# Edge numbers laid out on the host instead of turned on the chip, and the zeroing of the count matrix dealt out anew

## The reference

```
x = layernorm(x + sage(x, src, dst))        # two mean aggregations: h @ W_self + mean(h[src]) @ W_neigh + b
x = layernorm(x + mlp(x, edge_attr_64))     # message per edge: relu(relu([x[src], x[dst], attr] @ W1 + b1) @ W2 + b2), summed at dst
x = layernorm(x + gcn(x))                   # symmetric degree norm, self loops
x = layernorm(x + gin(x))                   # batch norm over the nodes
```

## Time and profile before

| what | value |
|---|---|
| median of 3 runs | 1707.18 us |
| the three runs | 1707.18, 1711.44, 1705.15 us |
| span of the profiled execution | 1708.6 us |
| end of phase 1 (first one-hot of the counting) | 27.80 us |
| end of the counting | 332.5 us |
| barrier before phase 5 | 498.5 us |
| busy in the span: PE, DVE, ACT, POOL | 1474.5, 753.7, 678.8, 773.8 us |
| mean granted TensorE clock | 0.949 of full |

### The profile page before, as it was taken

How to read it: one execution, slowest core, us unless ns; L and a number is a source line. 1 busy time by engine, 2 the same in 40 slices (tenths; PEclk the granted TensorE clock), 3 DMA queues, 4 the chain that set the end, 5 groups by cost and what they waited for, 6 DMA issues and landing times.

```text
span 1708.6 us, 31512 instructions
## 1 busy us (share of the span) xinstructions
PE 1474.5 (86%) x9804; PEld 1046.6 (61%) x9805; DVE 753.7 (44%) x2791; ACT 678.8 (40%) x1245; POOL 773.8 (45%) x821
## 2 busy tenths in 40 slices
PE   3789999999967877889898888889898888977997
PEld 2346666755555666667676667667666666654554
DVE  8987778622233322233234324333433343345445
ACT  7665555520012433344345334433444353331113
POOL 1300000000005777777777777777777777721000
PEclk9999999999987999989999999999999999988998
DMA  2000000000024333333333333333333333310001
GB/s 80 1 0 1 2 1 1 21 27 18 0 65 128 87 80 83 80 85 83 83 81 88 82 80 77 92 79 84 86 83 82 80 87 82 83 29 1 1 1 38
DMA packets 158749, 95.81 MB, mean 56 GB/s; under 512 B 120636, under 2 KB 143931, under 8 KB 158659
## 3 DMA queue, kind: packets, MB, share of 16 engines
q0 software_dynamic: 25088, 51.43, 11.9%
q1 hardware_dynamic: 133571, 43.21, 10.3%
HBM read 87.24 MB, written 7.32 MB: 55 GB/s over the span
## 4 chain that ended last, share of the span: by engine, by line
PE 33%; DMA 11%; POOL 9%; issue 7%; DVE 5%; DVEq 2%; ACT 2%; SPq 1%; POOLq 0%; ACTq 0%
DMA arena<-x_w1a,idx 10%; POOL arena L768 9%; PE ps L1093 6%; PE ps L1208 6%; PE ps L1102 5%; PE ps L1086 5%; PE ps L1074 3%; PE ps L1082 3%; PE ps L1143 2%; PE ps L1192 1%; DVEq L334 1%; DVE arena L2085 1%; DVE idx L2054 1%; DMA arena<-in_edge_attr 1%; ACT arena L1544 1%
## 5 line engine op out<-in xcount | busy, mean ns | idle before, releaser
L768 POOL DMA_INDIRECT arena<-x_w1a,idx x784 | 742.8, 947 | 684.1 <-issue 640.7
L1534 ACT ACTIVATE arena<-ps 88x512 f32<-88x512 f32 x196 | 116.2, 593 | 481.4 <-PE ps L1074 477.6
L1102 PEld LDWEIGHTS ps<-arena 128*128 128x128 f32 x1568 | 210.6, 198 | 111.8 <-issue 74.6
L2085 DVE TENSOR_TENSOR arena<-ps,bias_b 128x512 f32<-128x512 f32 x196 | 135.6, 692 | 208.1 <-PE ps L1093 208.1
L2080 DVE TENSOR_TENSOR arena<-win_i,late 128x96 f32<-128x96 f32 x196 | 51.1, 261 | 393.0 <-PE ps L1102 380.1
L1082 PE MATMUL ps<-ident_f,arena 128*128 128x128 f32 x784 | 131.2, 292 | 107.3 <-DMA arena<-x_w1a,idx 106.2
L1093 PE MATMUL ps<-w_c,arena 128*128 128x128 f32 x1568 | 222.2, 288 | 0.0
L1352 ACT ACTIVATE adj<-ps 128x300 f32 x392 | 172.1, 449 | 121.2 <-PE ps L831 114.4
L1086 PE MATMUL ps<-arena 88*128 88x512 f32 x392 | 210.1, 618 | 2.4 <-ACT arena L1534 2.4
L1093 PEld LDWEIGHTS ps<-w_c,arena 128*128 128x128 f32 x1568 | 205.4, 205 | 0.3
L1102 PE MATMUL ps<-arena 128*128 128x24 f32 x1568 | 199.3, 266 | 4.6 <-ACT arena L1544 1.4
(11 more groups left out here) (207 smaller groups left out, 1438.3 us busy)
## 6 DMA issues: line engine op xcount, KB each, us to landing
arena<-in_edge_attr SPq DMA_DIRECT2D x196, 128.0 KB
arena<-x_w1a,idx POOLq DMA_INDIRECT x784
arena<-x_w1b SPq DMA_DIRECT2D x196, 12.0 KB
x_spill<-arena SPq DMA_DIRECT2D x1, 1600.0 KB, 7.2
x_w1a<-arena SPq DMA_DIRECT2D x6, 256.0 KB, 2.3
x_w1b<-arena SPq DMA_DIRECT2D x6, 256.0 KB, 2.6
arena<-x_spill SPq DMA_DIRECT2D x6, 256.0 KB, 3.0
out_x<-arena SPq DMA_DIRECT2D x3, 512.0 KB
```

The costliest lines, as they stand in the source:

```text
L768: pool.indirect_dma_start(out=z_e[v][:, j * D:(j + 1) * D], out_offset=None, in_=xa_d[:, :], in_offset=bass.IndirectOffsetOnAxis(ap=idx[:, ...
L1102: last = pe.matmul(ps[:, WIN_BANK[v % 2], 0:WIN], msg[:, j * P:(j + 1) * P], oh_e[v][:, j, :], start=(j == 0), stop=(j == J - 1))
L2085: dve.tensor_tensor(msg.rearrange("p (j d) -> p j d", d=D), bank(5, J), over(bias_b, J), ALU.add).then_inc(m_sum[v], 1)
```

## The change

On the host, `src` and `dst` are padded to whole blocks and laid out with the edge position on the partitions, once for the counting and once for the later loop; first targets of half blocks, units and blocks are taken there too, and the node and edge features are padded with zero rows. On the chip, each of these is one transfer. The transposes, their copies, the store of the edge words and the patches of the last block go, and with them three semaphores. VectorE computes `high`, `low`, `rel`, `comb`, `lo_h` and the checks on 128 x 784 in place of 98 x 1024, and makes `drel` (the edge's target relative to its block) in phase 5 by one subtraction on 128 x 784. The raw numbers no longer stand in `adj`. Tiles are zeroed thus: VectorE 0 to 7 (was 0 to 6, 20, 21), ScalarE 8 to 16 (was 7 to 17, 22 to 24), GpSimd 17 to 24 in one instruction without a wait (was 18 and 19 behind `prep_ready`).

```diff
+def unit(q):
+    return 2 * (q // 4) + q % 2
+
+
+def unit_block(i, v, r):
+    return 2 * i + FB * r + FB * (v % 2) + v // 2
...
-        prep = adj[:, 20:25, :].rearrange("p k n -> p (k n)").bitcast(F32)
-        raw_src = prep[:, 0:1024].bitcast(I32)
-        raw_dst = prep[:, 1024:2048].bitcast(I32)
-        hi_i = prep[:, 2048:3072].bitcast(I32)
-        lo_i = prep[:, 3072:4096].bitcast(I32)
-        p_src = prep[:, 4096:5120]
-        p_lo = prep[:, 5120:6144]
-        p_drel = prep[:, 6144:7168]
-        p_comb = raw_dst.bitcast(F32)
-        p_rel = raw_src.bitcast(F32)
+        raw_src = arena[:, 10048:10048 + NB * J].bitcast(I32)
+        raw_dst = arena[:, 10832:10832 + NB * J].bitcast(I32)
+        high = arena[:, 11616:11616 + NB * J].bitcast(I32)
+        low = arena[:, 9024:9024 + NB * J].bitcast(I32)
+        rel = arena[:, 0:NB * J]
+        half_all = arena[:, 784:784 + HALVES].bitcast(I32)
...
-        edge_words = arena[:, 0:LATE]
-        src_words = edge_words[:, 0:J * (NB + 1)].bitcast(I32).rearrange("p (s j) -> p s j", j=J)
-        drel_words = edge_words[:, J * (NB + 1):LATE].rearrange("p (s j) -> p s j", j=J)
+        dst_words = late[:, J * (NB + 1):LATE].bitcast(I32)
+        base_all = arena[:, 10560:10560 + NB].bitcast(I32)
...
+        spans = [arena[0:1, 2800 + 200 * u:2800 + 200 * u + NB] for u in range(2)]
...
-            def block_rows(dst, src, s):
-                v = src[0:(NB - 1) * BLK].rearrange("(s e) -> s e", e=BLK)
-                sp.dma_start(dst[0:GRP, 0:512], v[0:GRP]).then_inc(s, 16)
-                sp.dma_start(dst[0:EVEN, 512:1024], v[GRP:GRP + EVEN]).then_inc(s, 16)
-                sp.dma_start(dst[EVEN:GRP - 1, 512:1024], v[GRP + EVEN:NB - 1]).then_inc(s, 16)
-                sp.dma_start(dst[GRP - 1:GRP, 512:1024],
-                             src[E - BLK:E].rearrange("(s e) -> s e", s=1)).then_inc(s, 16)
-
-            block_rows(raw_src, t["src"], loads[0])
-            block_rows(raw_dst, t["dst"], loads[1])
...
+            sp.dma_start(raw_src, t["src_counted"]).then_inc(loads[0], 16)
+            sp.dma_start(raw_dst, t["dst_counted"]).then_inc(loads[1], 16)
+            sp.dma_start(half_all, bcast(t["half_firsts"])).then_inc(loads[1], 16)
+            sp.dma_start(base_a, t["unit_firsts"]).then_inc(loads[2], 16)
+            sp.dma_start(base_row[:, :], t["block_firsts"].rearrange("(a s) -> a s", a=1)).then_inc(loads[2], 16)
 
             def load_nodes(dst, src, s):
-                sp.dma_start(dst[:, 0:NT - 1, :],
-                             src[0:(NT - 1) * P, :].rearrange("(k p) d -> p k d", p=P)).then_inc(s, 16)
-                sp.dma_start(dst[0:TAIL, NT - 1, :], src[(NT - 1) * P:N, :]).then_inc(s, 16)
-
-            sp.wait_ge(g_own, 1)
+                sp.dma_start(dst, src.rearrange("(k p) d -> p k d", p=P)).then_inc(s, 16)
+
             load_nodes(xn, t["x"], loads[3])
...
-            sp.wait_ge(loads[2], 112)
-            sp.wait_ge(prep_out, 8)
-            sp.wait_ge(prep_ready, 2)
-            sp.dma_start(late_d, edge_words).then_inc(words_moved, 16)
             phase_end(sp, 1)
             sp.wait_ge(adj_written, counted(ROUNDS))
-            sp.dma_start(late[:, :], late_d).then_inc(words_moved, 16)
+            sp.dma_start(base_all, bcast(t["block_firsts"])).then_inc(words_moved, 16)
+            sp.dma_start(dst_words, t["dst_edges"]).then_inc(words_moved, 16)
+            sp.dma_start(late[:, 0:J * (NB + 1)].bitcast(I32), t["src_edges"]).then_inc(words_moved, 16)
...
-            g.add(pool.memset(xn[:, NT - 1, :], 0.0))
...
-            pool.wait_ge(prep_ready, 1)
-            pool.memset(words(18, 20), 0)
+            pool.memset(words(17, 25), 0)
             phase_end(pool, 1)
...
-            pe.wait_ge(prep_ready, 1)
-            pe.wait_ge(g_own, 9)
-            n = 0
-            for half in range(2):
-                for a, v in enumerate((p_comb, p_lo, p_drel, p_src)):
-                    if n >= 2:
-                        pe.wait_ge(prep_out, n - 1)
-                    for j in range(J):
-                        c0 = 512 * half + j * P
-                        last = pe.transpose(ps[:, n % 2, GRP * j:GRP * (j + 1)], v[0:GRP, c0:c0 + P],
-                                            ident_f[0:GRP, 0:GRP])
-                    last.then_inc(prep_t, 1)
-                    n += 1
             phase_end(pe, 1)
...
-            zero(7, 12)
-            zero(12, 18)
-            for n in range(8):
-                half, a = n // 4, n % 4
-                dst = (comb, lo_h, drel_words, src_words)[a]
-                act.wait_ge(prep_t, n + 1)
-                act.activation(dst[:, GRP * half:GRP * (half + 1), :],
-                               ps[:, n % 2, 0:GRP * J].rearrange("p (j s) -> p s j", j=J), ACT.Copy
-                               ).then_inc(prep_out, 1)
-            zero(22, 25)
+            zero(8, 13)
+            zero(13, 17)
             phase_end(act, 1)
...
             dve.memset(cols[:, 6:7], 0.0).then_inc(cols_ready, 1)
             own.add(dve.memset(off[:, :], 0.0))
             dve.memset(words(0, 2), 0)
-            dve.wait_ge(loads[0], 64)
-            own.add(dve.tensor_scalar(hi_i[0:GRP, :], raw_src[0:GRP, :], 7, None, ALU.arith_shift_right))
-            own.add(dve.tensor_scalar(lo_i[0:GRP, :], raw_src[0:GRP, :], P - 1, None, ALU.bitwise_and))
-            own.add(dve.tensor_copy(p_src[0:GRP, :], raw_src[0:GRP, :]))
-            dve.wait_ge(loads[1], 64)
-            for half in range(2):
-                h = slice(512 * half, 512 * half + 512)
-                own.add(dve.tensor_scalar(p_drel[0:GRP, h], raw_dst[0:GRP, h],
-                                        raw_dst[0:GRP, 512 * half:512 * half + 1], None, ALU.subtract))
+            dve.wait_ge(loads[0], 16)
+            own.add(dve.tensor_scalar(high, raw_src, 7, None, ALU.arith_shift_right))
+            own.add(dve.tensor_scalar(low, raw_src, P - 1, None, ALU.bitwise_and))
+            dve.wait_ge(loads[1], 32)
+            firsts = half_all.rearrange("p (h a) -> p h a", a=1).broadcast_to([P, HALVES, J // 2])
+            own.add(dve.tensor_tensor(rel.rearrange("p (h j) -> p h j", j=J // 2),
+                                      raw_dst.rearrange("p (h j) -> p h j", j=J // 2), firsts, ALU.subtract))
             own.wait()
-            for h in range(4):
-                own.add(dve.tensor_scalar(p_rel[0:GRP, SUB * h:SUB * (h + 1)], raw_dst[0:GRP, SUB * h:SUB * (h + 1)],
-                                        raw_dst[0:GRP, SUB * h:SUB * h + 1], None, ALU.subtract))
-            firsts = raw_dst[0:GRP, :].rearrange("p (b h e) -> p b h e", h=2, e=SUB)[:, :, :, 0]
-
-            for c, x, y in ((4, 1, 0), (6, 0, 1)):
-                own.add(dve.tensor_tensor(off[0:GRP, c:c + 2], firsts[:, :, x], firsts[:, :, y], ALU.subtract))
-            own.add(dve.tensor_copy(p_lo[0:GRP, :], lo_i[0:GRP, :]))
-            own.wait()
-            dve.scalar_tensor_tensor(out=p_comb[0:GRP, :], in0=hi_i[0:GRP, :], scalar=float(WIN_A),
-                                     in1=p_rel[0:GRP, :], op0=ALU.mult, op1=ALU.add).then_inc(prep_ready, 1)
-            own.add(dve.tensor_reduce(off[0:GRP, 1:2], p_rel[0:GRP, :], mybir.AxisListType.X, ALU.max))
-            own.add(dve.tensor_reduce(off[0:GRP, 2:3], p_rel[0:GRP, :], mybir.AxisListType.X, ALU.min))
-            own.add(dve.tensor_scalar(off[0:GRP, 4:6], off[0:GRP, 4:6], float(WIN - WIN_A), None, ALU.subtract))
-            own.wait()
-            own.add(dve.tensor_scalar(off[0:GRP, 1:2], off[0:GRP, 1:2], WIN_A - 1.0, None, ALU.subtract))
-            own.add(dve.tensor_scalar(off[0:GRP, 2:3], off[0:GRP, 2:3], -1.0, None, ALU.mult))
-
-            dve.wait_ge(loads[2], 112)
+            own.add(dve.scalar_tensor_tensor(out=comb, in0=high.rearrange("p (s j) -> p s j", j=J), scalar=float(WIN_A),
+                                             in1=rel.rearrange("p (s j) -> p s j", j=J), op0=ALU.mult, op1=ALU.add))
+            own.add(dve.tensor_copy(lo_h, low.rearrange("p (s j) -> p s j", j=J)))
+            own.add(dve.tensor_reduce(off[:, 1:2], rel, mybir.AxisListType.X, ALU.max))
+            own.add(dve.tensor_reduce(off[:, 2:3], rel, mybir.AxisListType.X, ALU.min))
+            halves = half_all[0:1, :].rearrange("p (s h) -> p s h", h=2)
+            for u in range(2):
+                own.add(dve.tensor_tensor(spans[u], halves[:, :, 1 - u], halves[:, :, u], ALU.subtract))
+            dve.wait_ge(loads[2], 32)
             own.add(dve.tensor_tensor(falls, base_row[:, 0:NB - 1], base_row[:, 1:NB], ALU.subtract))
             own.add(dve.tensor_tensor(nears, base_row[:, 0:NB - APART], base_row[:, APART:NB], ALU.subtract))
             own.wait()
+            own.add(dve.tensor_scalar(off[:, 1:2], off[:, 1:2], WIN_A - 1.0, None, ALU.subtract))
+            own.add(dve.tensor_scalar(off[:, 2:3], off[:, 2:3], -1.0, None, ALU.mult))
+            for u in range(2):
```

(86 more changed lines are left out.)

## The result

Over all runs the changed kernel took 1716.74 us in the median (1714.60 to 1723.17, 7 runs) against 1709.16 us (1705.15 to 1711.44, 7 runs) for the kernel before: ratio **1.0051, 95% interval 1.0036 to 1.0065**, so 6 to 11 us slower. Forecast were 6.1 us more, most likely within 0.5%. The median lies inside the stated range by 0.3 us, but the kernel did move, to the slow side, and the start alone does not make up the difference.

The account below looks back on a forecast made before the run. VectorE was taken to bound the start, up to the first one-hot at 27.8 us. That one-hot coming 6.1 us later, all other terms nothing, added to the median 1707.2 gave 1713.3 us, range 1703 to 1717.

Parts of the forecast that it names:

- The hold: At the start, VectorE's shift `high` waits until GpSimd's 12,800-word fill ends at 14.7 us; VectorE stands 10.4 us.
- Both rivals that touch it: At the start: no hold or a short one (13%), 1703 to 1705 us; GpSimd's long fill slower per word (12%), 1715.8.
- VectorE's chain: At the start, VectorE's computation behind GpSimd's fill takes 8.6 us, then its fill 10.0 and the barrier 0.6.
- The shift passes to the end: From the first one-hot on, its delay reaches the end microsecond for microsecond; rival that it does not (5%): 1705 to 1712.
- the last block's window lies elsewhere, the same number of instructions: In the last block, at the program's end, the change costs nothing.
- The subtraction at 499 us: In front of the four index copies, 0.9 us more on VectorE, covered by 5.58 us idle for TensorE: nothing.
- a bound of 8.5: On the whole time, 0.5%, about what a measurement can tell from none; 81% chance of staying within it.
- A 15% share for slower: On the whole time, the chance given to the changed kernel being slower by more than 0.5%.

Follow-up runs that it names:

- The two experiments that take this row away: VectorE's fill first, and the changed kernel with GpSimd's fill waiting until VectorE's last wide copy: the latter 1706.76 us, ratio 0.9984.
- eight pieces: The changed kernel with GpSimd's fill of 12,800 words split into eight instructions of 1600: 1716.98 us, ratio 1.0037.
- VectorE's fill first: The changed kernel with VectorE filling all its eight tiles in one instruction before it computes anything: 1707.25 us, ratio 0.9988.
- rows of their own: The changed kernel with the last block's padding edges gathering rows 0 to 351, each its own: 1711.67 us, ratio 1.0004; three further versions build on it.
- the dealt one: The version with both edits, tiles redealt: VectorE 0 to 5, ScalarE 6 to 18, GpSimd 19 to 24: 1701.58 us, ratio 0.9941.
- the two profiles of the kernel before: The kernel before, and the kernel before with its 352 masked-out last-block edges gathering row 0: the latter 1710.98 us, ratio 1.0009.
- both edits: The changed kernel with VectorE's fill ahead of its computation and padding edges that gather a row each: 1703.20 us, ratio 0.9949.

## Why the prediction was right and wrong

- *The hold* was right, and nearly to the number: GpSimd's fill 3.45 to 14.21 us (forecast 3.6 to 14.7), the shift one row of 10.44 us ending with it. The two experiments that take this row away show that it costs the time: 9.9 and 9.0 us at the start, 0.63 and 0.67% of the whole. Both rivals that touch it are out: the hold is whole, and the long fill costs 0.841 ns a word, not more than the short one's 0.866.
- *VectorE's chain* with fill and barrier was 0.6 us cheaper than the sum, and GpSimd's fill ended 0.5 us earlier than forecast. From GpSimd's end to the last small scalar it took 14.21 to 22.4 = 8.2 us (8.6), the fill 10.0 (10.0), the barrier 0.43 (0.6). First one-hot 32.9 in place of 33.9, a shift of 5.1 in place of 6.1.
- *The shift passes to the end*: in three comparisons of versions that differ in the start only, 9.9, 9.9 and 9.0 us of start were worth 0.63, 0.55 and 0.67% (10.8, 9.4 and 11.4 us), each with an uncertainty of some 3 us. The first and the third cross sessions; within one, 10.2 us between the versions with eight pieces and with VectorE's fill first were worth 0.49% (8.4 us).
- **The step that failed** is the one on the last block, "the last block's window lies elsewhere, the same number of instructions", which the sum took at nothing. It counted instructions and did not ask what the padding edges fetch. The value 0 on the host made the last gathers read one row; they landed 1.5 us later, the wait grew from 1.44 to 2.98 us, and in the four versions that keep those rows (waits 2.94 to 3.18) TensorE ran behind it at the lower clock level: 17.3 to 19.1 us from last gather to last window sum, against 11.9 to 13.1 in three of the four with rows of their own (the fourth is the dealt one, below). By the ratios it is worth 0.39% and 0.47% in the two pairs that differ in nothing else, and 0.33% against the eight pieces; by the medians 4.1 to 5.4 us. That is 4 to 8 us. I had named work moved and its cover, not the data that it moves.
- *A gain I had not seen.* From the first one-hot to the first gather the two profiles of the kernel before took 494.2 and 494.3 us, the eight of changed kernels 490.1 to 492.4. Without it the changed kernel would stand at about +11 us. It has two parts, both behind the branch at the end of the counting. The first is a clock that is granted higher: the 75 matmuls behind the branch take 5.97 us before and 4.35 in six of the eight, 1.6 us. TensorE's idle in front of them is much the same (2.98 and 3.09 before, 2.51 to 2.94 changed), and why the changed kernels draw better there is open. The second lies in phase 5: from TensorE's first instruction of it to the first gather 20.9 and 20.6 us before, 19.1 to 19.4 in seven of the eight and 20.1 in the one with both edits. The clock alone does not explain that one: behind the wait for the stores eight matmuls take 2.04 us before and in the version with VectorE's fill first (19.3 us), and 1.13 in the other seven, the one with 20.1 among them. No run was made on either.
- *The subtraction at 499 us* took 0.97 us and was hidden: VectorE waited 5.00 us for TensorE behind the index copies, in place of 5.58.
- *The chances.* 6.1 us were set against a bound of 8.5 with most of the weight inside; the sum of +5.1 for the start, +4 to 8 for the end and -3 for the gain is 6 to 10, on both sides of the bound, and the +7.6 measured lies near the 6.1 in part because the gain offset the loss at the end: the closeness of the number is luck. A 15% share for slower was too little for a change that also altered data at the program's end.

## What to carry to other kernels

While GpSimd filled memory, a wide tensor_scalar on VectorE stood still to the end of the fills queued on GpSimd (10.4 to 10.7 us for half a microsecond of work); give VectorE its own fills in that time and its wide work after, and count a hold as part of the deal. Pad indices with distinct rows, above all in the last block, where nothing covers a late gather; in mid-loop the same delay cost nothing that shows here. And when a change moves padding to the host, ask what each padded element makes the chip do.

## What the hardware showed that was not expected

- Eight fills of 1600 words on GpSimd held VectorE's instruction for 10.70 us, as one of 12,800 did (10.44): there was no turn between them.
- A one-column tensor_scalar ran in 0.15 us inside GpSimd's fill; a two-column one had taken 0.68, held to the fill's end.
- Gathers in which all partitions fetch one row made TensorE wait 2.67 to 3.18 us, against 2.04 at most elsewhere in the ten traces; TensorE started 4.2 to 5.2 us behind the block's last issue, against 2.8 in the median.
- The clock level behind a wait is not fixed by its length: 2.51 us of idle was followed by 5.97 us for 75 matmuls in one version, 2.94 us by 4.35 in two others. In the dealt version the last stretch fell to a granted clock of 0.65 with no long wait in front, and took 15.6 us.
